# Adding the two expert rows of a token in PSUM, and sharing out the end of a mixture-of-experts layer

## The reference

```python
abel_out = gelu(xn @ abel_w + abel_b)
topw, topi = top_k(xn @ moe_gate_w + moe_gate_b, 2); topw = softmax(topw)
h = gelu(einsum('bsd,edh->ebsh', xn, ew1) + eb1)
eo = einsum('ebsh,ehd->ebsd', h, ew2) + eb2
moe_out = sum over the two chosen experts of topw * eo
for i in range(3): moe_out = moe_out @ expm(gens[i])
gate = sigmoid(concatenate([abel_out, moe_out]) @ gc_w + gc_b)
mixed = abel_out * (1 - gate) + moe_out * gate
out = layernorm(z + residual + mixed)
```

## Time and profile before

| | us |
|---|---|
| three runs | 752.81, 751.75, 750.41 |
| their median | 751.75 |
| the profiled execution, its own time | 751.09 |
| its span, first to last instruction | 749.2 |
| PE busy | 640.8 (86%) |
| DVE busy | 593.1 (79%) |
| ACT busy | 455.9 (61%) |
| POOL busy | 243.7 (33%) |

### The profile page before, as it was taken

One profiled execution on the slowest core, in us unless ns is written; L12 is line 12 of the kernel. 1 busy time (PEld: TensorE's weight loads), 2 busy tenths in 40 slices (PEclk: granted clock), 3 DMA queues, 4 the chain that ended last, 5 costly groups with the idle time before them and its releaser, 6 DMA issues. The chain is left out here.

```text
span 749.2 us, 16171 instructions
## 1 busy us (share of the span) xinstructions
PE 640.8 (86%) x4525; PEld 470.1 (63%) x4526; DVE 593.1 (79%) x1543; ACT 455.9 (61%) x868; POOL 243.7 (33%) x295
## 2 busy tenths in 40 slices
PE   5789999999998999999989985799999999997000
PEld 4657557466574746657574864588888888886000
DVE  4878778899998989999798865577777777784593
ACT  3156483955648295564938342677777777784187
POOL 2003020214427062442606422034343433344042
PEclk9999999999999999999999999799999999999555
DMA  4643232164733536373845642466656555410873
GB/s 142 210 126 56 85 54 60 57 141 169 144 113 91 137 115 141 107 149 126 217 111 168 235 151 64 109 159 163 149 143 161 146 120 146 97 49 12 278 256 140
DMA packets 124502, 99.21 MB, mean 132 GB/s; under 512 B 60432, under 2 KB 114587, under 8 KB 124316
## 3 DMA queue, kind: packets, MB, share of 16 engines
q1 hardware_dynamic: 108028, 68.82, 32.1%
q0 software_dynamic: 16416, 29.67, 16.9%
HBM read 62.42 MB, written 33.68 MB: 128 GB/s over the span
## 5 line engine op out<-in xcount | busy, mean ns | idle before, releaser
L1831 POOL DMA_INDIRECT scratch_ys<-ye,place x78 | 82.9, 1063 | 155.1 <-ACT ye L1877 143.2
L58 PE MATMUL up<-xe_s,words 128*128 128x256 bf16 x936 | 112.3, 278 | 13.2 <-DVE xe_s L1981 13.2
L58 PE MATMUL bank<-words 128*128 128x512 bf16 (+1 forms) x576 | 109.2, 343 | 6.8 <-DVE logits L1022 4.1
L58 PE MATMUL down<-words,h_s_e 128*128 x936 | 110.4, 274 | 3.9 <-DVE yb L1965 3.8
L58 PEld LDWEIGHTS up<-xe_s,words 128*128 x936 | 93.3, 100 | 26.3 <-issue 13.9
L58 PEld LDWEIGHTS down<-words,h_s_e 128*128 128x128 bf16 x936 | 90.2, 98 | 19.1 <-issue 6.5
L58 PE MATMUL bank<-xn_s,mlp_w 128*128 128x512 bf16 x384 | 88.3, 383 | 2.5 <-DVE xn_s L747 2.5
L58 PEld LDWEIGHTS bank<-words 128*128 128x128 bf16 x576 | 55.1, 98 | 54.0 <-issue 7.6
L58 PE MATMUL bank<-mlp_w,shared 128*128 128x256 bf16 x768 | 86.4, 273 | 0.0
L476 POOL DMA_INDIRECT scratch_zs<-rows,pos x64 | 71.5, 1117 | 42.7 <-DVE pos L1072 24.0
L58 PEld LDWEIGHTS bank<-mlp_w,shared 128*128 128x128 bf16 x768 | 75.0, 98 | 10.6 <-issue 0.4
(11 more groups left out here) (243 smaller groups left out, 1152.3 us busy)
## 6 DMA issues: line engine op xcount, KB each, us to landing
xb<-scratch_zs SPq DMA_DIRECT2D x156, 64.0 KB
words<-scratch_ys SPq DMA_DIRECT2D x16, 514.0 KB, 8.7
scratch_abel<-staged SPq DMA_DIRECT2D x8, 514.0 KB, 5.0
abel_all<-scratch_abel SPq DMA_DIRECT2D x8, 514.0 KB
x_in<-in_x SPq DMA_DIRECT2D x8, 512.0 KB, 5.1
words<-in_out_b_row SPq DMA_DIRECT2D x8, 512.0 KB, 3.7
x_res<-in_mlp_b_row SPq DMA_DIRECT2D x8, 512.0 KB, 3.5
words<-in_x POOLq DMA_DIRECT2D x8, 512.0 KB, 7.8
```

Source lines behind the costliest of these rows:

```text
L58: last = nc.tensor.matmul(dst, lhs(a, k), rhs(b, k), start=start and n == 0, stop=stop and n == total - 1)
L1831: nc.gpsimd.indirect_dma_start(out=ys_dram[:, :], out_offset=bass.IndirectOffsetOnAxis(ap=place[:, k, s:s + 1], axis=0), in_=ye[:, k % 2, ...
```

## The change

In the loop, PE signals `down_done` behind each 128 rows, and `biased` waits for each of them by itself. All waits on `down_done` are scaled to match.

In the end: SP loads batch 0 in halves, tiles 0 and 1 of both rows first (`half_in`), then tiles 2 and 3; DVE adds and subtracts these halves separately. DVE runs mixed(0) ahead of differ(1). For batches 1 to 7 PE adds the two rows: for each tile two f32 matmuls with the identity as stationary operand, the second accumulating on the first (`sums`), into PSUM banks b % 2 * 4 to + 3; it may run two batches ahead of DVE's `differ`. `differ(b)` is then one subtraction, with PSUM as its first input. DVE finishes one tile of four by itself (two of four in the last two batches) with a two-operation instruction, and ACT the others; each has its semaphore (`res_v`, `res_r`), and who waited for a finished batch now waits for both. On ACT spreads(0) moves ahead of gates_of(1). The six PSUM tensors become slices of one of 8 banks.

```diff
-        up_bank = [[pb(f"up{i}{j}", [P, 2, SLOT]) for j in range(2)] for i in range(2)]
-        down_bank = [pb(f"down{n}", [P, 512]) for n in range(ST)]
+        banks = pb("banks", [P, 8, 512])
+        up_bank = [[banks[:, 2 * i + j].rearrange("p (c n) -> p c n", c=2) for j in range(2)] for i in range(2)]
+        down_bank = [banks[:, 4 + n] for n in range(ST)]
...
+        def act_tiles(b):
+            return range(TT - 1 if b < BATCHES - 2 else TT - 2)
+
+        def vector_tiles(b):
+            return range(len(act_tiles(b)), TT)
+
+        def finished_by_act(b):
+            return sum(len(act_tiles(k)) for k in range(b + 1))
+
+        def finished_by_vector(b):
+            return sum(len(vector_tiles(k)) for k in range(b + 1))
+
+        def wait_finished(eng, b):
+            wait(eng, res_r, finished_by_act(b))
+            wait(eng, res_v, finished_by_vector(b))
...
-                sp.wait_ge(res_r, TT * (b + 1))
+                wait_finished(sp, b)
...
-            sp.wait_ge(down_done, QT)
+            sp.wait_ge(down_done, ST * QT)
             for k, s in enumerate(ys_out):
                 sp.wait_ge(s, 16 * ST * len(range(k, QT, 4)))
-            for b in range(BATCHES):
+            for r in range(2):
+                sp.dma_start(got[:, 0, r, 0:TT // 2], ys_v[r, 0][:, 0:TT // 2]).then_inc(half_in, 16)
+            for r in range(2):
+                sp.dma_start(got[:, 0, r, TT // 2:TT], ys_v[r, 0][:, TT // 2:TT]).then_inc(got_in[0], 16)
+            for b in range(1, BATCHES):
                 for r in range(2):
                     sp.dma_start(got[:, b, r], ys_v[r, b]).then_inc(got_in[b], 16)
...
             def gates_of(b):
-                act.wait_ge(diff_r, b + 1)
+                act.wait_ge(diff_r, b + 2)
...
-                for n in range(TT):
+                for n in act_tiles(b):
                     nc.scalar.activation(got[:, b, 0, n, 0:D], mix[:, b % MIX, n], ACT.Identity,
                                          bias=shift[:, b % 2, n:n + 1], scale=rs[:, b % 2, n:n + 1]).then_inc(res_r, 1)
...
             gates_of(0)
+            spreads(0)
             for b in range(BATCHES):
                 if b + 1 < BATCHES:
                     gates_of(b + 1)
-                spreads(b)
+                if b > 0:
+                    spreads(b)
                 if b > 0:
                     finished(b - 1)
             finished(BATCHES - 1)
...
-                dve.wait_ge(down_done, q + 1)
                 wait(dve, ye_r, ST * (q - 1))
                 for n in range(ST):
+                    dve.wait_ge(down_done, ST * q + n + 1)
                     nc.vector.tensor_tensor(yb[:, par, n], down_bank[n][:, 0:DG], ebias[:, bass.ds(e * DG, DG)],
                                             ALU.add).then_inc(yb_r, 1)
...
-                dve.wait_ge(got_in[b], 32)
                 wait(dve, mix_r, TT * (b - 1))
                 wait(dve, gate_r, b - 1)
-                nc.vector.tensor_tensor(diff[:, b % 2], got[:, b, 0], got[:, b, 1], ALU.add).then_inc(both_r, 1)
-                dve.wait_ge(both_r, b + 1)
-                nc.vector.tensor_tensor(diff[:, b % 2], diff[:, b % 2], abel[:, b], ALU.subtract).then_inc(diff_r, 1)
+                if b == 0:
+                    for h, loaded in enumerate((half_in, got_in[0])):
+                        at = slice(h * TT // 2, (h + 1) * TT // 2)
+                        dve.wait_ge(loaded, 32)
+                        nc.vector.tensor_tensor(diff[:, 0, at], got[:, 0, 0, at], got[:, 0, 1, at], ALU.add)\
+                            .then_inc(both_r, 1)
+                        dve.wait_ge(both_r, h + 1)
+                        nc.vector.tensor_tensor(diff[:, 0, at], diff[:, 0, at], abel[:, 0, at], ALU.subtract)\
+                            .then_inc(diff_r, 1)
+                else:
+                    dve.wait_ge(sum_r, TT * b)
+                    nc.vector.tensor_tensor(diff[:, b % 2], banks[:, b % 2 * TT:b % 2 * TT + TT, 0:DG], abel[:, b],
+                                            ALU.subtract).then_inc(diff_r, 1)
+
+            def finished(b):
+
+                dve.wait_ge(shift_r, b + 1)
+                for n in vector_tiles(b):
+                    nc.vector.tensor_scalar(got[:, b, 0, n, 0:D], mix[:, b % MIX, n], rs[:, b % 2, n:n + 1],
+                                            shift[:, b % 2, n:n + 1], ALU.mult, ALU.add).then_inc(res_v, 1)
...
-                wait(dve, res_r, TT * (b - MIX + 1))
+                wait_finished(dve, b - MIX)
...
                 dve.wait_ge(rs_r, b + 1)
-                wait(dve, res_r, TT * (b - 1))
+                wait_finished(dve, b - 2)
                 nc.vector.tensor_tensor(shift[:, b % 2], less_mean[:, b % 2], rs[:, b % 2], ALU.mult).then_inc(shift_r, 1)
...
             differ(0)
+            mixed(0)
             differ(1)
-            mixed(0)
             for b in range(BATCHES):
                 if b + 2 < BATCHES:
                     differ(b + 2)
                 if b > 0:
                     shifts(b - 1)
+                    finished(b - 1)
                 if b + 1 < BATCHES:
                     mixed(b + 1)
                 variances(b)
             shifts(BATCHES - 1)
+            finished(BATCHES - 1)
...
@@ -2066,7 +2108,7 @@
                     last = split_product(nc, down_bank[n][:, 0:DG],
                                          lambda s, k: h_s[:, par, s, k, n * P:(n + 1) * P],
                                          lambda s, k: w2_s[:, s, bass.ds(e * (FC * DG) + k * DG, DG)], FC)
-                last.then_inc(down_done, 1)
+                    last.then_inc(down_done, 1)
...
+            def sums(b):
+                wait(pe, diff_r, b if b > 2 else 0)
+                pe.wait_ge(got_in[b], 32)
+                for n in range(TT):
+                    nc.tensor.matmul(banks[:, b % 2 * TT + n, 0:DG], ident[:, :], got[:, b, 0, n], start=True, stop=False)
+                    nc.tensor.matmul(banks[:, b % 2 * TT + n, 0:DG], ident[:, :], got[:, b, 1, n], start=False, stop=True)\
+                        .then_inc(sum_r, 1)
+
             over_tiles(pe, body)
             down(QT - 1, (QT - 1) % 4, expert_of(QT - 1))
+            pe.wait_ge(yb_r, ST * QT)
+            for b in range(1, BATCHES):
+                sums(b)
```

More of the change, by code:

```diff
@@ L1740, in experts @@
         got_in = [sem(f"c_got_in{k}") for k in range(BATCHES)]
+        half_in, sum_r, res_v = sem("c_half_in"), sem("c_sum_r"), sem("c_res_v")
         out_stored = sem("c_out_stored")
@@ L1838, in rstd @@
                 pool.wait_ge(ve_r, b + 1)
-                wait(pool, res_r, TT * (b - 1))
+                wait_finished(pool, b - 2)
                 nc.gpsimd.tensor_tensor(rs[:, b % 2], ve[:, b % 2], neg_half[:, 0:TT], ALU.pow).then_inc(rs_r, 1)
@@ L1969, in split_hidden @@
                 par = k % 2
-                wait(dve, down_done, q - 1)
+                wait(dve, down_done, ST * (q - 1))
                 for c in range(0, FC, 2):
```

## The result

| | before | after | forecast |
|---|---|---|---|
| median of 14 runs each, same chip | 752.64 us | 748.61 us | 745.8 (743.8 to 748.6) |
| ratio, 95% interval | | 0.9951 (0.9936 to 0.9967) | 0.992 |
| span of the profiled execution | 749.2 | 745.2 | 743.5 |
| first load of expert rows | 695.20 | 690.18 | 694.8 |
| from there to the end of the span | 54.0 | 55.0 | 48.7 |

Faster by 0.5%, just outside the range, and by a stretch to which the forecast had given next to nothing. Everything that was to be gained lay behind the first load of expert rows, and there the kernel became 1.0 us *longer*. 5.0 us were won ahead of that load, where I had put 0.4.

What follows compares the result with a forecast made beforehand. DVE was taken to set the pace in the end, ACT close behind. Of 5.7 us off the span (749.2 to 743.5), 3.1 came from turns and 2.6 from sharing the last tiles; forecast 745.8 us, range 743.8 to 748.6.

Steps and rivals of the forecast that it cites:

- the term for the loop: Loop tiles other than the last: 0 gained, ends -1.5 and +0.5 us, as PE works without a break.
- the price of an f32 matmul: PE's row additions, 128x257 f32: 0.43 us each at the low clock, 0.225 at the full clock.
- the hand-over of the last tile: Loop's last tile: only one bias of 0.38 us stays on the path to scatter and loads, -0.4 us.
- The bound of 2.6 us: Loop: PE busy 197.36 of 200 us, so only speeding DVE there can bring no more than 2.6 us.
- the loop's moving by more than 1 us: Loop: a stated sign that the prediction is wrong, if its length moves by more than 1 us.
- The estimate from the four passes: PE's additions by the skill's figure: 0.43 us a matmul at 2.4 GHz, 0.86 at 1.2; span end about 767.
- only the bytes ahead of batch 1 count: Loads in the end: halving batch 0 leaves the bytes up to batch 1 the same, so it lands at 703.3.
- A turn, 3.77: DVE's turn per batch in the end: 4.57 - 1.26 + 0.10 + 0.36 = 3.77 us, ends 3.65 and 4.0.
- the rival of the held power: Turns 1 to 5: shift waits 0.9 us for POOL's power, losing 4.5 of 5.7; about 750.5, chance 0.09.
- The way out: From differ(7)'s start D: last ACT tiles at D+12.1, the store's 4.0 us leaves D+16.1, span end 743.5.
- The last one: Gain mostly the loop's or not there: 0.3 us a turn over 7 turns, 748.1 us, chance 0.09.
- The slow PE: End: PE becomes the bound above 0.53 us per matmul; at 0.77, about 765 us, chance 0.05.

Runs made afterwards that it cites:

- dve_adds_all: Changed kernel with DVE adding the rows of all batches in two passes; 747.70 us beside 746.77 for the kernel before, ratio 1.0019.
- the early start: Run alone: kernel before with only down products signalled and awaited per 128 rows; ratio 0.9934 on one chip, 1.0009 and 0.9989 on two others.

## Why the prediction was wrong, point by point

Three steps failed: the term for the loop, put at 0; the price of an f32 matmul, half of what it is; and the cause of the last 4.0 us. In the profiled execution they add up as follows, measured less forecast: the first load -4.6, from there to turn 1 +4.7, the turns -0.1, from differ(7) to the end +1.8, in all, before rounding, the 1.7 between 745.2 and 743.5. The other 1.1 of the miss of 2.8 is the distance of the median from the profiled execution, 1.5 where I had taken 0.4.

- **The loop, "I take 0 there".** It was worth 4.4 us and the hand-over of the last tile 0.6: all of the gain, with 1.0 lost again behind. Two readings failed. The bound of 2.6 us was taken from busy time, which runs on behind each stop. And the waits were judged one by one ("DVE waits less, but PE works without a break"), when the earlier trace rows itself said that PE had breaks, and in the long loops its breaks go with DVE's waits. The last tile's hand-over was near the forecast of 0.4: from the end of the last down product to the first load it took 5.40 (690.18 - 684.78) against 5.98 (695.20 - 689.22), 0.6 less. The prediction named the loop's moving by more than 1 us as a sign of being wrong, and it moved by 4.4.
- **The price of an f32 matmul, "0.43 each at the low clock, 0.225 at the full".** Half of what it is. The trace writes an f32 matmul as two records, and I counted records as matmuls. The rows gave it away: the fold has 8 experts x 4 parts x 2 = 64 calls at L1504, and the kernel before has, beside the 64 records that I took, these:

```profile
L1504 PE MATMUL bank<-turnmat,raw x48: 377/379/484, 430.7 to 460.0; 128*128 128x257 f32 x48
L1504 PE MATMUL bank<-turnmat,shared x16: 377/520/677, 444.1 to 449.1; 128*128 128x257 f32 x16
```

  128 in all. The change's 56 calls are 112 records, x56 on each of its two lines. So 0.43 is the price at the full clock and about 0.86 at the low one. The estimate from the four passes that the Trainium skill states (FP8 and Floating Point Precision, section TensorE Precision Notes) was the same 0.43 and 0.86, and the trace agrees with it. It spoke against the change, I had both numbers side by side, and the one from the trace was the misread one. Sums(1) and (2) took 5.2 and 3.6 us instead of 3.6 and 2.1. That is 3.1 of the 4.7 us by which turn 1 came late, 22.1 from the first load instead of 17.45. Another 1.4 is that PE began 9.9 from the first load instead of 8.5. The prediction had argued that only the bytes ahead of batch 1 count. But the chain of waits has two more issues on SP ahead of its transfer (2.5 us to it instead of 1.5), and the transfer took 7.3 instead of 7.0.
- **A turn, 3.77.** Right to 0.02 in the mean, and each of its terms to 0.04: the pass from PSUM 1.23, a tile on DVE 0.33, POOL's power 1.01 to 1.04, no wait. In the kernel before, beside passes with both inputs in SBUF, the power took 1.94 to 1.98, so the reason given against the rival of the held power stands. That differ(7) began at 727.3, as forecast, is luck: 4.6 too early at the load, 4.7 too late in turn 1.
- **The way out, "the store's 4.0".** The distance from ACT's last tile to the end was right in the trace and wrong as a cause. What lay 7.7 us behind the last power was POOL's drain. ACT's last tile did come earlier (12.5 us from differ(7), against 14.7 before and 12.1 forecast), and that bought nothing: the end is 17.9 behind differ(7) where 16.1 was forecast and 18.7 was before, and the 0.8 less is what the last power's start moved (10.2 from differ(7) against 11.0).
- **The rivals.** None named the drain. The last one had "the gain is mostly the loop's" in its title, but no reason for it and no price; what it summed was a wait of ACT in each turn, and its 748.1 lies near the measured 748.61 by luck. The slow PE had the right mechanism at the wrong price: 0.43 in the turns is under the 0.53 from which it would decide, but the first two batches are paid in full. Since the end was 1.0 us worse in the profiles and what lies ahead of it 5.0 better, the sum came out near the forecast for wrong reasons.

## What to carry to other kernels

Before a row's "mean of one" becomes a price, divide its count by the calls in the code; f32 matmuls are two records each. Where engines wait for each other, many small waits on the engine off the path can go with a slower loop: an earlier signal took them away here and cost nothing that the runs show (1.0009 and 0.9989 where there was nothing to gain), and counts of instructions in equal windows showed the loss where busy shares didn't. And look at each engine's closing instructions before taking the last store for the end: a short operation on an engine with a long drain belongs early, or elsewhere, and what it gains ends at the next bound (1.0 us here).

## What was not expected of the hardware

- POOL's closing drain takes 7.50 us (7499 to 7502 ns) in all twenty profiles, from the start of its last power on; SP's takes 7 ns and those of the other engines 0.2 to 4.1 us (8 ns in one case, PE's in dve_adds_all). What it waits for no run tells.
- The same kernel ran its loop in 214.1 us on one chip and in 218.7 and 220.1 on two others, one profile each, with medians of 746 and 751 to 753. Two chips are two measurements, and the early start gained 0.66% on one and nothing on two others.
- PE kept the full clock through 23 us of additions at 0.43 us each without a gap. It had it 3.0 us after the first one in `after`, 3.0 to 6.0 over the ten profiles, and with that PE's first batch took 5.0 to 6.5 us.
